# The last feed-forward of a two-layer transformer kernel: sums kept in the maxima banks, and the engines' orders written anew

## What is computed

```python
x = L0_attn_x                                     # (4, 256, 256) f32
x = _layernorm(x + _L0_attn_ref(x, ...))          # 32 query heads, 8 kv heads
x = _layernorm(x + _L0_ffn_ref(x, ...))           # fp8-rounded weights, inner size 768, silu
x = _layernorm(x + _L1_attn_ref(x, ...))          # 16 query heads, 8 kv heads
x = _layernorm(x + _L1_ffn_ref(x, ...))           # weights looked up in a table of 16, inner size 688

def _layernorm(x, axis=-1, eps=1e-05):
    m = jnp.mean(x, axis=axis, keepdims=True)
    v = jnp.var(x, axis=axis, keepdims=True)
    return (x - m) / jnp.sqrt(v + eps)
```

## Time and profile before

| | |
|---|---|
| median of 3 runs | 363.53 us (360.98 to 364.22) |
| profiled execution | 362.06 us |
| its span, first to last instruction | 360.2 us |
| TensorE busy | 299.7 us, 83% |
| VectorE busy | 258.1 us, 72% |
| ScalarE busy | 246.3 us, 68% |
| GpSimd busy | 195.2 us, 54% |
| mean granted TensorE clock | 0.92 |

### The profile page before, as it was taken

The page is one execution under the profiler, slowest core; times in us unless marked ns, Lnnn a source line. Parts: engine busy times, 40 slices in busy tenths (PEclk is TensorE's granted clock), DMA queues, the critical chain, the costliest instruction groups (busy, mean ns, idle before and its releaser), DMA issues.

```text
span 360.2 us, 7105 instructions
## 1 busy us (share of the span) xinstructions
PE 299.7 (83%) x2608; PEld 198.9 (55%) x2608; DVE 258.1 (72%) x399; ACT 246.3 (68%) x449; POOL 195.2 (54%) x261
## 2 busy tenths in 40 slices
PE   8446127687869897998979999999999999999990
PEld 7334002222426462564535765687778887979990
DVE  7695999898889897999986676656754657416341
ACT  3766677988588868797677776687677636654340
POOL 5756562404195348983398422564664346528763
PEclk9858555879899999999999999999999999999996
DMA  6468571201331000230001650032013000000000
GB/s 196 135 159 208 151 237 29 89 23 51 100 92 48 5 5 25 67 95 0 24 5 39 189 181 4 1 85 52 0 32 105 0 5 31 1 2 31 0 31 29
DMA packets 24872, 23.06 MB, mean 64 GB/s; under 512 B 3542, under 2 KB 24838, under 8 KB 24838
## 3 DMA queue, kind: packets, MB, share of 16 engines
q1 hardware_dynamic: 24838, 22.61, 22.2%
HBM read 10.47 MB, written 3.26 MB: 38 GB/s over the span
## 4 chain that ended last, share of the span: by engine, by line
PE 58%; DVE 13%; POOL 8%; ACT 8%; issue 7%; SPq 4%; DMA 2%; POOLq 0%; DVEq 0%; ACTq 0%
PE FB L1236 16%; PE PV L1179 9%; PE FB L1249 8%; PE MM L1124 6%; DVE LV L1042 5%; DVE MX L950 5%; PE SC L1158 4%; PE FB L1208 3%; PE SC L1153 2%; ACT PB L838 2%; PE FB L1078 2%; PE FB L1191 2%; SPq L542 2%; DMA QS<-QP 2%; ACT LV L885 2%
## 5 line engine op out<-in xcount | busy, mean ns | idle before, releaser
L950 DVE TENSOR_REDUCE MX<-MM 128x4 f32<-128x1024 f32 x96 | 117.0, 1219 | 40.1 <-PE MM L1124 39.5
L838 ACT ACTIVATE PB<-SC 128x1024 f32<-128x1024 f32 x96 | 98.2, 1023 | 31.7 <-PE SC L1153 19.5
L1124 PE MATMUL MM<-KS,QS 62*128 62x256 bf16 (+1 forms) x384 | 47.5, 292 | 33.6 <-DVE MX L950 24.8
L1179 PE MATMUL PV<-PB,VP 128*32 128x256 f32 x768 | 61.8, 408 | 1.3 <-ACT PB L838 1.3
L706 POOL TENSOR_TENSOR HL<-HF,HH 128x256 fp32r<-128x256 f32 (+1 forms) x48 | 37.6, 787 | 45.0 <-ACT HH L815 45.0
L1124 PEld LDWEIGHTS MM<-KS,QS 62*128 62x128 bf16 (+1 forms) x384 | 19.4, 97 | 59.4 <-DVE MX L950 39.4
L1042 DVE COPY_PREDICATED LV<-LB,LV 128x1728 f32<-128x1728 uint8 (+2 forms) x30 | 42.6, 1419 | 3.5 <-POOL LV L724 3.1
L1236 PE MATMUL FB<-XH,W 128*128 128x256 f32 x192 | 42.9, 305 | 0.5 <-DVE HF L1002 0.5
L1236 PE MATMUL FB<-XL,W 128*128 128x256 f32 x192 | 38.5, 282 | 0.0
L999 DVE SCALAR_TENSOR_TENSOR AA<-TH,FB 128x256 f32<-128x256 f32 (+1 forms) x48 | 20.0, 416 | 22.4 <-ACT TH L829 19.6
L1153 PE MATMUL SC<-QS,KS 64*128 64x256 bf16 x256 | 26.5, 287 | 9.8 <-ACT PB L838 7.8
(11 more groups left out here) (96 smaller groups left out, 578.5 us busy)
## 6 DMA issues: line engine op xcount, KB each, us to landing
QS<-QP SPq DMA_DIRECT2D x48, 128.0 KB, 2.4
IX<-in_idx SPq DMA_DIRECT2D x10, 216.0 KB, 4.0
dw<-LO SPq DMA_DIRECT2D x10, 216.0 KB, 2.1
W1L<-dw SPq DMA_DIRECT2D x10, 216.0 KB, 3.8
KS<-KP SPq DMA_DIRECT2D x24, 64.0 KB, 2.0
XT<-in_xt SPq DMA_DIRECT2D x4, 256.0 KB, 3.0
X<-in_x SPq DMA_DIRECT2D x4, 256.0 KB, 4.0
out<-X SPq DMA_DIRECT2D x4, 256.0 KB, 2.1
```

The lines of the kernel that those rows point to most:

```text
L838: act.activation(PB[:, quad % PB_QUADS, kt, :, :], SC[:, :, :], ACT.Exp, scale=DH[layer(j)] ** -0.5).then_inc(exp_done, 1)
L950: dve.tensor_reduce(mx, MM[:, :, :].rearrange("p (f i) s -> p f i s", f=2), axis=AX.X, op=ALU.max).then_inc(max_red, 1)
L1124: ins = pe.matmul(MM[:, 2 * f + i, :], QS[lo:lo + r, j % NST, qs + h, qt * P:(qt + 1) * P], keys(j)[lo:lo + r, j % NST, ks, :], start=True ...
L1179: ins = pe.matmul(PV[32 * c:32 * c + 32, r % 2, :], v, PB[:, quad % PB_QUADS, kt, place(j, c), :], start=part == 0, stop=part == (3, 1)[la ...
```

## The change

Job 7, the last one, treats its feed-forward sums otherwise. Each tile of 128 tokens has its own PSUM bank, one of the two that held the maxima, and the products of a chunk are made tile by tile. ScalarE's copy and GpSimd's addition (`down.7` of ScalarE, `dsum.7`) go: VectorE adds the bank to X, takes the statistics and adds eps for one tile and then for the other; GpSimd makes only the power, one column for each tile; VectorE normalizes in a new step `fin`; and SyncE stores each tile by itself. In all 16 norms the mean is subtracted as it is, so NM and its step go. All five tables are rewritten, with the same steps otherwise; TensorE's has 540 before and after.

```diff
                     j = step[1]
+                    if j == JOBS - 1:
+                        for t in range(TT):
+                            sp.wait_ge(x_last, t + 1)
+                            sp.dma_start(out[batch(j), t * P:(t + 1) * P, :], X[:, batch(j), t, :]).then_inc(out_wr, 16)
+                        continue
...
+                    if step == ("down", JOBS - 1):
+
+                        for t in range(TT):
+                            pool.wait_ge(var_last, t + 1)
+                            pool.tensor_tensor(RSTD[:, n % 2, t:t + 1], VE[:, n % 2, t:t + 1], NHALF[:, 0:1],
+                                               ALU.pow).then_inc(rstd_last, 1)
+                        continue
                     pool.wait_ge(mv_done, n + 1)
-                    pool.tensor_scalar(NM[:, n % 2, :], MV[:, n % 2, :, 0], -1.0, 0.0, ALU.mult, ALU.add)
                     link(pool.tensor_scalar(VE[:, n % 2, :], MV[:, n % 2, :, 1], 1.0, EPS, ALU.mult, ALU.add))
                     link(pool.tensor_tensor(RSTD[:, n % 2, :], VE[:, n % 2, :], NHALF[:, :], ALU.pow))
                     for t in range(TT):
-                        ins = pool.tensor_scalar(X[:, batch(j), t, :], X[:, batch(j), t, :], NM[:, n % 2, t:t + 1],
-                                                 RSTD[:, n % 2, t:t + 1], ALU.add, ALU.mult)
+                        ins = pool.tensor_scalar(X[:, batch(j), t, :], X[:, batch(j), t, :],
+                                                 MV[:, n % 2, t, 0:1], RSTD[:, n % 2, t:t + 1], ALU.subtract, ALU.mult)
...
+                    n = norms[step]
+                    dve.wait_ge(x_new, n - 1)
+                    for t in range(TT):
+                        dve.wait_ge(down_half, t + 1)
+                        link(dve.tensor_tensor(X[:, b, t, :], X[:, b, t, :], MM[:, 2 * t, :], ALU.add))
+                        link(dve.bn_stats(BST[:, n % 2, t, :], X[:, b, t, :]))
+                        link(dve.bn_aggr(MV[:, n % 2, t, :], BST[:, n % 2, t, :]))
+                        dve.tensor_scalar(VE[:, n % 2, t:t + 1], MV[:, n % 2, t, 1:2], 1.0, EPS, ALU.mult,
+                                          ALU.add).then_inc(var_last, 1)
+                elif kind == "fin":
+
+                    b = batch(JOBS - 1)
+                    n = norms["down", JOBS - 1]
+                    for t in range(TT):
+                        dve.wait_ge(rstd_last, t + 1)
+                        dve.tensor_scalar(X[:, b, t, :], X[:, b, t, :], MV[:, n % 2, t, 0:1], RSTD[:, n % 2, t:t + 1],
+                                          ALU.subtract, ALU.mult).then_inc(x_last, 1)
...
+                    if j == JOBS - 1:
+
+                        if i == 0:
+                            pe.wait_ge(max_red, unit0(JOBS))
+                        for t in range(TT):
+                            for k, (part, hs) in enumerate(products):
+                                ins = pe.matmul(MM[:, 2 * t, :], hs[0:rows(l, i), i, t * P:(t + 1) * P],
+                                                ffn_down(l, i)[part], start=i + k == 0,
+                                                stop=(i, k) == (5, len(products) - 1))
+                            if i == 5:
+                                ins.then_inc(down_half, 1)
+                        continue
```

Of the tables, the places that the text speaks of. TensorE's beginning and its end from the last context on:

```diff
-        "q.0.0@0 q.0.1 kv.0.0@1 kv.0.1 kv.1.0@2 kv.1.1 q.1.0@0 q.1.1 max.0.0 q.2.0@1 q.2.1 q.3.0@0 q.3.1 max.0.1 "
+        "q.0.0@0 kv.0.0@1 kv.0.1 kv.1.0@2 kv.1.1 q.0.1 q.1.0@1 q.1.1 max.0.0 q.2.0@0 q.2.1 q.3.0@1 q.3.1 max.0.1 "
...
-        "pv.7.3.1 back.7.0@2 down.5.5 turn.7.1@1 wo.7.0@2 gu.6.1.0@0 back.7.1@1 gu.6.1.1 wo.7.1 gu.6.2.0@1 gu.6.2.1 "
-        "gu.6.3.0@0 gu.6.3.1 gu.6.4.0@2 gu.6.4.1 gu.6.5.0@1 gu.6.5.1 down.6.0@0 down.6.1 down.6.2 down.6.3 tr.7.0@2 "
-        "down.6.4 down.6.5 gu.7.0.0@1 gu.7.0.1 gu.7.1.0@2 gu.7.1.1 gu.7.2.0@0 gu.7.2.1 gu.7.3.0@1 gu.7.3.1 gu.7.4.0@2 "
+        "back.7.0@2 down.5.5 turn.7.1@0 wo.7.0@2 gu.6.0.0@1 back.7.1@0 gu.6.0.1 wo.7.1 gu.6.1.0@0 gu.6.1.1 gu.6.2.0@1 "
+        "gu.6.2.1 gu.6.3.0@2 gu.6.3.1 gu.6.4.0@0 gu.6.4.1 gu.6.5.0@1 gu.6.5.1 down.6.0@2 down.6.1 down.6.2 tr.7.0@0 "
+        "down.6.3 down.6.4 down.6.5 gu.7.0.0@1 gu.7.0.1 gu.7.1.0@0 gu.7.1.1 gu.7.2.0@2 gu.7.2.1 gu.7.3.0@1 gu.7.3.1 "
```

VectorE's beginning, and around the norm `down.0`:

```diff
-        "scales lutbits.0 q8.0 lut2.0 q8.1 max.0.0 lut3.0 lut4.0 q8.2 lutbits.1 max.0.1 max.0.2 q8.3 max.0.3 lut2.1 "
+        "scales lutbits.0 q8.0 lut2.0 q8.1 lut3.0 lut4.0 max.0.0 lutbits.1 q8.2 max.0.1 max.0.2 lut2.1 max.0.3 q8.3 "
...
-        "lut2.6 max.2.5 gu.0.3 lut3.6 max.2.6 gu.0.4 max.2.7 gu.0.5 mt.2.0 max.2.8 turn.1.0 max.2.9 turn.1.1 lut4.6 "
-        "down.0 max.2.10 lutbits.7 max.2.11 max.2.12 wo.1 max.2.13 lut2.7 lut3.7 max.2.14 lut4.7 max.2.15 lutbits.8 "
+        "gu.0.2 max.2.5 gu.0.3 lut3.6 max.2.6 gu.0.4 lut4.6 max.2.7 gu.0.5 mt.2.0 max.2.8 turn.1.0 lutbits.7 max.2.9 "
+        "turn.1.1 max.2.10 down.0 max.2.11 lut2.7 max.2.12 lut3.7 max.2.13 lut4.7 wo.1 max.2.14 lutbits.8 max.2.15 "
```

SyncE's beginning:

```diff
-        "ldxt.1 ldq8.0 ldq8.1 ldix.0 ldix.1 load.0 ldix.2 qstack.0.1 qstack.0.0 qstack.0.2 ldq8.2 kstack.0.0 "
-        "kstack.0.1 kstack.0.2 ldxt.2 ldxt.3 ldx.0 qstack.1.0 ldq8.3 qstack.1.1 load.1 qstack.1.2 ldix.3 kstack.1.0 "
+        "ldxt.1 ldq8.0 ldq8.1 ldix.0 ldix.1 load.0 ldix.2 qstack.0.0 qstack.0.1 kstack.0.0 ldq8.2 qstack.0.2 "
+        "kstack.0.1 kstack.0.2 ldxt.2 ldxt.3 load.1 qstack.1.0 qstack.1.1 ldq8.3 kstack.1.0 qstack.1.2 kstack.1.1 "
```

More of the change, by code:

```diff
@@ L345, in two_layer_kernel @@
         MV = sb("MV", [P, 2, TT, 2])
-        NM = sb("NM", [P, 2, TT])
         RSTD = sb("RSTD", [P, 2, TT])
@@ L412, in two_layer_kernel @@
         x_new = sem("x_new")
+        x_last = sem("x_last")
+        var_last = sem("var_last")
+        rstd_last = sem("rstd_last")
+        down_half = sem("down_half")
         th_done = sem("th_done")
@@ L611, in _ @@
                                  X[:, batch(j), :, :]).then_inc(out_wr, 16)
-            sp.wait_ge(out_wr, 16 * B)
+            sp.wait_ge(out_wr, 16 * (B + TT - 1))
         @block.gpsimd
@@ L987, in _ @@
                     b = batch(j)
-                    dve.wait_ge(x_sum, j + 1)
-                    layer_norm(b, step)
+                    if j < JOBS - 1:
+                        dve.wait_ge(x_sum, j + 1)
+                        layer_norm(b, step)
+                        continue
+                    n = norms[step]
[14 more added lines that the diff above has]
+                                          ALU.subtract, ALU.mult).then_inc(x_last, 1)
                 elif kind == "gu":
```

## The result

The changed kernel took 377.54 us (median of 4 runs, 374.65 to 379.74), beside 363.29 for the kernel before on the same chip (4 runs, 360.98 to 364.22): a ratio of 1.040, with a 95% interval of 1.031 to 1.049. It is slower by some 14 us, where 358.5 was forecast and 364.5 was the upper end. Its profiled execution took 378.48, with a span of 376.7.

What follows compares the result with a forecast made beforehand. No engine is full from 60 to 180 us; TensorE sets the end from 180, then a serial tail. Tail -2.4, mean 0, orders -2.6 sum to -5.0 us, from the median of 363.53 to 358.5, range 354.8 to 364.5.

Steps and rivals of the forecast that it cites:

- The mean: Norms on GpSimd: dropping NM saves some 0.27 us each, subtraction costs what addition did; counted 0, at most 0.8 us gain.
- part two of the prediction: The part on the mean: NM goes from all 16 norms; counted as 0.
- The cover that I named: For 15 norms, TensorE's transpose of X stands behind 5.6 to 10.7 us of other work after the output projection.
- The tail: Last matmul to end: 5.8 us instead of 8.17; -2.1 us from the chain, -0.3 from the store, together -2.4.
- The orders: Rewritten tables of all engines, same steps in other places: -2.6 us taken, ends a loss of +5 and -5.5.
- The sum over stretches between reductions: Longer of VectorE's and TensorE's durations over 95 stretches: 277.8 us old, 271.8 new, -6.0, of which -4.1 left.
- a sum with ScalarE: Same sum over stretches between two exponentials, with ScalarE and TensorE: -3.3 us, less 1.4 left behind, -1.9.
- The rival that named ScalarE as the gate: 60 to 180 us: late exponentials hold TensorE's scores, waits more than double, 367.0 us; chance 0.10 with other such losses.
- the forecast's own signs of failure: Reduction waits reappearing under ScalarE's name or as DMA waits, or early order gain returning as TensorE idle in jobs 5-7.
- The first reduction: Start of the kernel: first maxima some 0.3 us later, inside 2.92 us of slack; within 0.5 us of 22.28.
- The rivals: Orders worth nothing: 361.1 us, chance 0.22; tail not delivering: 362.9, 0.08; ScalarE as gate: 367.0, 0.10 with similar losses.

Runs made afterwards that it cites:

- e1: Kernel before with old orders and tail; only NM and its step go, and GpSimd subtracts the mean from MV: 376.76 us, 1.040 of before.
- e4: Kernel before with old orders and the addition of NM kept, and only the new tail: 360.12 us, 0.994 of before.
- e16: Kernel before with new tail, addition kept, old orders to max.2.1 except max.0.13 to max.1.11 on TensorE, new orders behind: 364.27 us, 1.005 of before.
- e2: Changed kernel (new orders and new tail) with NM and its addition restored in the 15 norms on GpSimd: 364.20 us, 1.006 of before.
- e7: Edit of e2: in SyncE's queue the rows of mt.0.1 go ahead of the load ldq8.11: 364.87 us, 1.007 of before.
- e13: Kernel before with new tail, addition kept, new orders to max.0.13 on TensorE, old to max.2.1, new behind: 360.01 us, 0.994 of before.
- e5: Kernel before with new tail, addition of NM kept, old orders to max.2.1 and new ones behind: 359.45 us, 0.992 of before.

## Why the prediction was wrong

**The mean: wrong, and the step that failed.** "The subtraction costs what the addition did" had no row. The trace of before has no two-operation instruction on GpSimd with a subtraction, and yet it was given one price and no bounds. In part two of the prediction this term stood at 0, between 0 and a gain of 0.8. It is 1.22 us a tile undisturbed against 0.55, 0.67 more for each of 30 tiles, against 0.27 saved in each norm. The cover that I named, 5.6 to 10.7 us of other work, was real for most transposes and too thin for six to eight of them: 14.7 us (e1), measured alone. "If that cover is gone it is a gain still" was wrong with it. By this the forecast would have been missed whatever the rest did.

**The tail: right.** 5.56 us for 5.8, and 1.9 us of gain alone (1.0 to 3.2 by e4's interval) for 2.4. Its terms: addition from PSUM 0.42 (0.424 forecast); statistics 0.43, aggregate 0.18, VE 0.15 (0.40, 0.17, 0.17); last normalization 0.41 (0.42, the upper of its bounds); power of one column 0.57, and 0.66 for the second, which ran beside tile 0's normalization (0.71 for both). VectorE's subtraction costs what an addition costs there; GpSimd's does not. The Trainium skill (SBUF — State Buffer, "Who interferes with whom") has the two engines exclude one another on their shared ports; by that the normalization at 373.29 in a two-port mode would have kept the power off until 373.69, and a power of 0.57 would have ended at 374.26. The trace has it start at 373.45, last 0.09 longer and end at 374.11, so it does not show the power kept off; in which mode the normalization ran is not shown.

**The orders: wrong in sign for the first third, no gain shown behind it.** The sum over stretches between reductions counted each engine's own steps and took the longer. It gave a gain of 6.0, cut to 2.6; measured are 4.1 lost. That it matched the old order within 1% was no proof for the new one. My reading, which no run tests, is that the old order has the steps which feed one another in the right places, so that in a stretch little but its own work counts. The sum can't see a step of VectorE that waits for one of TensorE that stands behind another that waits for ScalarE: 3.1 us of VectorE's work (the copy, the turn's norm and a reduction) was 5.02 long in e16. I did run a sum with ScalarE, but again as durations between exponentials and not as a chain. The rival that named ScalarE as the gate came nearest: an exponential and a copy in the wrong place hold the turn. But TensorE's waits for exponentials did not double; 7.9 us in e2 for 7.8 before. The wait is VectorE's own, for TensorE's turn, and TensorE's waits for reductions were even fewer (20.5 us in e2 for 24.8). Of the forecast's own signs of failure, waits under ScalarE's name missed it, and waits for DMA rose (4.2 us for the rows in e2, 2.0 before) but e7, where that wait is 2.2 us, is no faster. Nor did the sum know that TensorE's steps take longer at the lower clock, which made some 2.5 of the 5.2 us that e16 is behind at max.1.12.

**The first reduction: wrong.** It started 2.2 us later (24.5), where 0.3 within a slack of 2.9 was forecast. It cost next to nothing (e13), since what followed caught up.

**The rivals.** None had this outcome. The slower side was held by ScalarE's gate at 367.0. With the addition in place (e2, 1.006 of before, or 365.5 us beside the first result's 363.29) the kernel would have ended between the rivals, and still just above the range.

The lowest time of all kernels here is e5's: new tail, the addition kept, the old orders to max.2.1 and the new ones behind. It takes 359.45 us, 0.8% less than before (interval 0.4 to 1.1), where 1.4% was forecast for the change, and the noise doesn't part it from e4, which has the new tail alone.

## What to carry to other kernels

An instruction that changes its operation is a new instruction: where no row shows that operation on that engine, bound it by a factor of two at least and multiply by its count before calling it free, and measure it alone if that product exceeds what the change can win. An order is not the sum of the longest engine in each stretch: follow, for each step that moved, what it waits for on the other engines and what is queued behind it, above all an in-order engine that has such a step ahead of the one that sets the pace. When new tables lose, cut them where both have done the same steps: six kernels with spliced tables found the part that single swaps had not. And price TensorE's steps at the clock that the stretch is granted.

## What was not expected of the hardware

GpSimd's tensor_scalar with two operations on 128 x 256 f32 takes 0.55 us with add and mult and 1.22 with subtract and mult or mult and subtract (on the mean of whole runs 0.64 to 0.69 and 1.33 to 1.41), with the scalar operand contiguous or every second number. Its two-tensor subtraction shows nothing of it: on 128 x 512 the subtraction XL and the addition X both take 1.27 us in the kernel before. VectorE does the same subtract and mult in 0.41 us. And TensorE, kept busy for 8.1 of 10 us by added matmuls, had a granted clock of 0.50 all the same.
